# Top-k attention: the exponent moves into the evacuation of transposed blocks, GpSimd scales, scores are kept two pairs ahead

## The reference

```python
scores = jnp.einsum('bhnd,bhmd->bhnm', q, k) * DHEAD ** (-0.5)
kth = jax.lax.top_k(scores, TOPK)[0][..., -1:]            # TOPK = 64
masked = jnp.where(scores >= kth, scores, jnp.finfo(scores.dtype).min)
attn = jax.nn.softmax(masked, axis=-1)
o = jnp.einsum('bhnm,bhmd->bhnd', attn, v)
...
o = _conv1x1(o, Wo, bo) + x
```

## Time and profile before

| | us |
|---|---|
| median of 3 runs | 5220.38 |
| lowest and highest | 5220.33 and 5223.14 |
| span of the profiled execution, first to last instruction | 5216.1 |

### The profile page before, as it was taken

The page is one execution under the profiler, slowest core; times in us unless marked ns, Lnnn a source line. Parts: engine busy times, 40 slices in busy tenths (PEclk is TensorE's granted clock), DMA queues, the critical chain, the costliest instruction groups (busy, mean ns, idle before and its releaser), DMA issues. The chain is left out here.

```text
span 5216.1 us, 112540 instructions
## 1 busy us (share of the span) xinstructions
PE 4171.7 (80%) x32161; PEld 2822.7 (54%) x32161; DVE 4319.4 (83%) x25277; ACT 4144.4 (79%) x6082; POOL 1502.1 (29%) x362
## 2 busy tenths in 40 slices
PE   8576677776776667766777777898999999999999
PEld 4344445444444344444555445443567777777776
DVE  4899899998999899989999999531378888888886
ACT  2798799988998788988999889644267887778785
POOL 0344345443454344444444444200100000000000
PEclk9677777777777677767777777899899999999999
DMA  6000000000000000000000000200320101011112
GB/s 211 6 18 16 7 17 17 8 17 14 11 17 17 7 17 8 17 16 8 17 18 8 17 16 8 65 6 0 151 73 25 35 25 34 25 34 33 26 34 93
DMA packets 79613, 154.90 MB, mean 30 GB/s; under 512 B 8120, under 2 KB 49464, under 8 KB 73528
## 3 DMA queue, kind: packets, MB, share of 16 engines
q1 hardware_dynamic: 78904, 146.72, 9.8%
HBM read 99.50 MB, written 47.19 MB: 28 GB/s over the span
## 5 line engine op out<-in xcount | busy, mean ns | idle before, releaser
L542 POOL TENSOR_TENSOR a_probs<-a_scores,a_probs 128x2304 f32<-128x2304 f32 x288 | 1460.2, 5092 | 1728.3 <-ACT a_probs L465 1728.3
L560 DVE MAX8 a_top<-a_scores 128x8 f32<-128x36 f32 x18432 | 1831.1, 180 | 47.0 <-ACT a_scores L449 47.0
L376 PE MATMUL a_ps_t<-ident,a_probs 128*128 128x128 f32 x5184 | 974.7, 326 | 646.7 <-ACT a_probs_t L460 520.1
L376 PEld LDWEIGHTS a_ps_t<-ident,a_probs 128*128 128x128 f32 x5184 | 673.9, 164 | 934.5 <-ACT a_probs_t L460 656.4
L465 ACT ACTIVATE a_probs<-a_scores,a_steep_kth 128x2304 f32<-128x2304 f32 x290 | 641.2, 2211 | 242.3 <-DVE a_minus_max L696 242.3
L1159 PE MATMUL b_ps_t<-ident,b_soft 128*128 128x128 f32 x5184 | 748.4, 280 | 20.5 <-issue 18.6
L1284 DVE TENSOR_SCALAR_CACHE_REDUCE b_soft<-b_ps_s 128x2304 f32<-128x2304 f32 x288 | 735.3, 2553 | 28.4 <-PE b_ps_s L1143 10.4
L460 ACT ACTIVATE a_probs_t<-a_ps_t 128x512 f32<-128x512 f32 (+1 forms) x1440 | 726.9, 545 | 22.3 <-PE a_ps_t L376 7.9
L1159 PEld LDWEIGHTS b_ps_t<-ident,b_soft 128*128 128x128 f32 x5184 | 583.2, 142 | 205.7 <-issue 80.6
L1241 ACT ACTIVATE b_soft<-b_soft,b_minus_max 128x2304 f32<-128x2304 f32 x288 | 638.1, 2216 | 41.6 <-issue 24.4
L366 PE MATMUL a_ps_s<-a_k_stack,a_q_ring 128*128 128x512 f32 (+1 forms) x1465 | 651.7, 604 | 14.2 <-ACT a_scores L449 9.6
(11 more groups left out here) (134 smaller groups left out, 4149.7 us busy)
## 6 DMA issues: line engine op xcount, KB each, us to landing
a_k_stack<-k_parts SPq DMA_DIRECT2D x72, 288.0 KB, 6.0
b_k_stack<-k_parts SPq DMA_DIRECT2D x72, 288.0 KB, 6.0
a_q_ring<-q_parts SPq DMA_DIRECT2D x294, 64.0 KB
b_q_ring<-q_parts SPq DMA_DIRECT2D x294, 64.0 KB
k_parts<-p_high SPq DMA_DIRECT2D x36, 256.0 KB, 2.1
k_parts<-p_rest SPq DMA_DIRECT2D x36, 256.0 KB, 2.1
q_parts<-p_high SPq DMA_DIRECT2D x36, 256.0 KB, 2.0
q_parts<-p_rest SPq DMA_DIRECT2D x36, 256.0 KB, 2.0
```

The source lines that it names most:

```text
L376: last = pe.transpose(ps_t[(NTG * s + g) % 2][:, P * m:P * m + P], probs[s % 2][:, P * (m0 + m):P * (m0 + m) + P], cst["ident"][:, :])
L542: pool.tensor_tensor(probs[u][:, :], scores_all[:, 2 * (p % 2) + u, :], probs[u][:, :], ALU.subtract).then_inc(masked_ready, 1)
L560: last = dve.max(top8[s // 2 % 2][:, s % 2, c, :], scores_all[:, s % 4, CHUNK * c:CHUNK * c + CHUNK])
```

## The change

`exponentials` no longer works in place: GpSimd, after its mask, adds `minus_max` (now the plain negative maximum) and multiplies by SCALE in place, and signals `shifted_ready`; TensorE transposes that, and ScalarE's evacuation of a transposed group is an Exp instead of a Copy. The row's sum comes out of TensorE: `v_s` has 32 columns of ones beside V, so that `weigh` has 64 output columns, two neighbouring blocks write two halves of `ps_o`, and `add_quadrants` brings 33 columns, the last of which is the sum. `o_top` holds 33 columns a head, and `project_out` divides out of it into a new tile. Scores are made and kept two tiles further ahead: `score(s + 6)` and `(s + 7)` instead of `(s + 5)` and `(s + 6)`, `keep_scores(s + 6)` and `(s + 7)` at the end of ScalarE's iteration instead of `(s + 4)` and `(s + 5)` inside it. The counts of doubts move to unused columns of `ps_s`. The core of the diff:

```diff
-        v_s = [sb(f"v{n}", [P, MCH, D]) for n in range(2)]
+        v_s = [sb(f"v{n}", [P, MCH, 2 * D]) for n in range(2)]
...
-                    rows = slice(D * (m % 4), D * (m % 4) + D)
+                    rows = slice(2 * D * (m % 2), 2 * D * (m % 2) + 2 * D)
                     last = pe.matmul(ps_o[rows, P * (s % 2):P * (s % 2) + P], v_s[s // MCH][:, m, :], probs_t[:, m, :],
-                                     start=m < 4, stop=m + 4 >= MCH)
+                                     start=m < 2, stop=m + 2 >= MCH)
...
-                    last = pe.matmul(ps_o[:, O_COL + D * u:O_COL + D * u + D], parts[:, P * u:P * u + P],
+                    first = O_COL + (D + 1) * u
+                    last = pe.matmul(ps_o[:, first:first + D + 1], parts[:, P * u:P * u + P],
                                      cst["add_up"][:, :], start=True, stop=True)
...
             count_doubts(0)
+            score(5, 0, 5)
...
-                    pe.wait_ge(probs_ready, tile + 1)
+                    pe.wait_ge(shifted_ready, tile + 1)
                     turn(s, 0, tile)
                     turn(s, 1, tile)
-                    score(s + 5, h, tile + 5)
                     if p % PAIRS == 0:
                         pe.wait_ge(v_ready, h * B + p // PAIRS + 1)
                     pe.wait_ge(parts_ready, pair + 1)
                     weigh(s, 0, tile)
                     turn(s, 2, tile)
+                    weigh(s, 1, tile)
                     turn(s, 3, tile)
-                    weigh(s, 1, tile)
+                    score(s + 6, h, tile + 6)
+                    weigh(s, 2, tile)
                     turn(s, 4, tile)
-                    weigh(s, 2, tile)
                     weigh(s, 3, tile)
-                    pe.wait_ge(probs_ready, tile + 2)
+                    pe.wait_ge(shifted_ready, tile + 2)
                     turn(s + 1, 0, tile + 1)
                     weigh(s, 4, tile)
+                    turn(s + 1, 1, tile + 1)
+                    weigh(s + 1, 0, tile + 1)
+                    turn(s + 1, 2, tile + 1)
                     count_doubts(pair + 1)
-                    turn(s + 1, 1, tile + 1)
-                    turn(s + 1, 2, tile + 1)
-                    weigh(s + 1, 0, tile + 1)
+                    weigh(s + 1, 1, tile + 1)
                     turn(s + 1, 3, tile + 1)
-                    weigh(s + 1, 1, tile + 1)
+                    weigh(s + 1, 2, tile + 1)
                     turn(s + 1, 4, tile + 1)
-                    for g in range(2, NTG):
-                        weigh(s + 1, g, tile + 1)
+                    weigh(s + 1, 3, tile + 1)
+                    weigh(s + 1, 4, tile + 1)
                     add_quadrants(pair)
-                    score(s + 6, h, tile + 6)
+                    score(s + 7, h, tile + 7)
...
-            def keep_turned(s, g, tile):
+            def exponentials(s, g, tile):
+
                 m0, n = TGROUPS[g]
                 act.wait_ge(turned, tile * NTG + g + 1)
                 act.activation(probs_t[:, m0:m0 + n, :],
                                ps_t[(NTG * s + g) % 2][:, 0:n * P].rearrange("p (m q) -> p m q", q=P),
-                               ACT.Copy).then_inc(turned_kept, 1)
+                               ACT.Exp).then_inc(turned_kept, 1)
...
-                    exponentials(s, h, tile, parity)
-                    keep_scores(s + 4, tile + 4)
+                    exponentials(s, 0, tile)
                     guess_place(1, pair + 1, 1 - parity)
-                    keep_turned(s, 0, tile)
-                    keep_turned(s, 1, tile)
-                    exponentials(s + 1, h, tile + 1, parity)
-                    keep_turned(s, 2, tile)
-                    keep_turned(s, 3, tile)
-                    keep_turned(s, 4, tile)
-                    keep_scores(s + 5, tile + 5)
+                    exponentials(s, 1, tile)
+                    exponentials(s, 2, tile)
+                    exponentials(s, 3, tile)
+                    exponentials(s, 4, tile)
+                    exponentials(s + 1, 0, tile + 1)
+                    exponentials(s + 1, 1, tile + 1)
                     keep_any(pair + 1)
-                    keep_turned(s + 1, 0, tile + 1)
-                    keep_turned(s + 1, 1, tile + 1)
+                    exponentials(s + 1, 2, tile + 1)
+                    exponentials(s + 1, 3, tile + 1)
                     act.wait_ge(kth_ready, pair + 2)
                     penalty(0, 1 - parity)
-                    keep_turned(s + 1, 2, tile + 1)
-                    keep_turned(s + 1, 3, tile + 1)
-                    keep_turned(s + 1, 4, tile + 1)
+                    exponentials(s + 1, 4, tile + 1)
                     penalty(1, 1 - parity)
                     act.wait_ge(weighed, tile + MCH + 3)
                     act.activation(parts[:, :], ps_o[:, 0:PAIR], ACT.Copy).then_inc(parts_ready, 1)
                     guess_place(0, pair + 2, parity)
+                    wait_alone(act, masked_ready, tile + 3)
+                    keep_scores(s + 6, tile + 6)
                     finish(s, h, pair)
+                    wait_alone(act, masked_ready, tile + 4)
+                    keep_scores(s + 7, tile + 7)
...
                     for u in range(2):
-                        pool.wait_ge(penalty_ready, tile + u + 1)
+
+                        wait_alone(pool, penalty_ready, tile + u + 1)
                         pool.tensor_tensor(probs[u][:, :], scores_all[:, 2 * (p % 2) + u, :], probs[u][:, :],
                                            ALU.subtract).then_inc(masked_ready, 1)
+                        wait_alone(pool, masked_ready, tile + u + 1)
+                        pool.tensor_scalar(probs[u][:, :], probs[u][:, :], minus_max[p % 2][:, u:u + 1], SCALE,
+                                           ALU.add, ALU.mult).then_inc(shifted_ready, 1)
...
-                dve.tensor_tensor(o_c, o_c, inverse_c, ALU.mult).then_inc(divided, 1)
+                dve.tensor_tensor(o_c, o_heads[:, 4 * c:4 * c + 4, :, 0:D], inverse_c, ALU.mult).then_inc(divided, 1)
```

More of the change, by code:

```diff
@@ L84, in constants @@
         "ones": sb("ones", [P, P]),
-        "add_up": sb("add_up", [P, D]),
+        "add_up": sb("add_up", [P, D + 1]),
     }
-    made = ctx.enter_context(nc.semaphore("constants_made"))
+    made, zeroed = ctx.enter_context(nc.semaphore("constants_made")), ctx.enter_context(nc.semaphore("ident_zeroed"))
     Tally.semaphore = ctx.enter_context(nc.semaphore("waits_alone"))
@@ L92, in _ @@
         def _(pool):
-            pool.memset(k["ident"][:, :], 0.0).then_inc(made, 1)
-            pool.wait_ge(made, 1)
+            pool.memset(k["ident"][:, :], 0.0).then_inc(zeroed, 1)
+            pool.wait_ge(zeroed, 1)
             pool.affine_select(out=k["ident"][:, :], in_=k["ident"][:, :], compare_op=ALU.not_equal,
                                fill=1.0, base=0, pattern=[[-1, P]],
-                               channel_multiplier=1).then_inc(made, 1)
+                               channel_multiplier=1).then_inc(made, 2)
         @block.vector
@@ L101, in _ @@
             dve.memset(k["ones"][:, :], 1.0)
[L102 to L106, removed]
+            dve.memset(k["add_up"][:, :], 0.0).then_inc(made, 1)
+            dve.wait_ge(made, 3)
+            for half in range(2):
+                values, total = 2 * D * half, 2 * D * half + D
+                dve.tensor_copy(k["add_up"][values:values + D, 0:D], k["ident"][values:values + D, values:values + D])
+                dve.tensor_copy(k["add_up"][total:total + D, D:D + 1], k["ident"][total:total + D, total:total + 1])
     return k
@@ L309, in attention_top @@
         ps_o = ctx.enter_context(nc.psum_tensor("a_ps_o", [P, BANK], F32))
-        O_COL, FLAG_COL = PAIR, PAIR + 2 * D
+        flag_counts = ps_s[0:1, N:N + 3]
+        O_COL = PAIR
         v_ready = sem("v_ready")
@@ L318, in attention_top @@
         kth_ready = sem("kth_ready")
-        penalty_ready, masked_ready, probs_ready = sem("penalty_ready"), sem("masked_ready"), sem("probs_ready")
+        penalty_ready, masked_ready, shifted_ready, ones_set = (sem("penalty_ready"), sem("masked_ready"),
+                                                                sem("shifted_ready"), sem("ones_set"))
         turned, turned_kept = sem("turned"), sem("turned_kept")
@@ L392, in count_doubts @@
                 pe.wait_ge(doubt_ready, pair + 1)
-                pe.matmul(ps_o[0:1, FLAG_COL:FLAG_COL + 2], cst["ones"][:, 0:1], doubt[:, :], start=True, stop=True)
+                pe.matmul(flag_counts[:, 0:2], cst["ones"][:, 0:1], doubt[:, :], start=True, stop=True)
                 for u in range(2):
-                    last = pe.matmul(ps_o[0:1, FLAG_COL + 2:FLAG_COL + 3], cst["ones"][:, 0:1], doubt[:, u:u + 1],
+                    last = pe.matmul(flag_counts[:, 2:3], cst["ones"][:, 0:1], doubt[:, u:u + 1],
                                      start=u == 0, stop=u == 1)
@@ L498, in _ @@
             act.wait_ge(kth_ready, 1)
```

(15 more changed lines are left out.)

25 lines of the change are left out of this document (13 added, 12 removed).

## The result

The changed kernel takes 6484.3 us (median of four runs, 6481.2 to 6488.9) against 5221.8 for the kernel before: a ratio of 1.242, 95% interval 1.240 to 1.244. The span of the profiled execution is 6482.1 us. The prediction was 6650, its range 5900 to 7250.

A forecast was written before the change was run, and what follows sets the result against it. ScalarE and VectorE, both nearly full, were taken to bound the kernel before; after, a ring through GpSimd's masks. 9.9 us times 143 pairs plus 10 for the start, added to 5220, gave about 6650 us, range 5900 to 7250.

The forecast's parts named there:

- the ring: Attention loop: GpSimd's masks and the TensorE-ScalarE exchange take turns, as late keepings wait for masks; 30.75 us a pair against 20.82.
- Step 1: From the end of penalty(0), GpSimd does mask 0, scale 0 and mask 1 while ScalarE ends up waiting: 13.15 us.
- Step 2: ScalarE after mask 1: keep_scores(s+7), exponentials(s,0), guess_place, exponentials(s,1), with scale 1 running under it: 4.3 us.
- Step 3: TensorE alternates turns and weighs up to turn(s+1,3), plus a score and count_doubts: 9.0 us at full clock, 13.3 at half.
- 10 for the start: The first iteration of the loop also waits for mask 1: about 10 us, once.
- 1.26 were carried: Mean pair minus ordinary pair before the change, from pairs counted again: 1.26 us, 180 us in all, taken as unchanged.
- Step 4: ScalarE's exponentials(s+1,3) with its handover, then penalty(0), before GpSimd's next mask: 3.0 us.
- Signs: In the changed profile: ScalarE idle 6 to 7 us a pair, GpSimd 13 to 15, evacuations 1.1 to 2 us apart.
- Hidden work: VectorE's select and the threshold some 2 us later end about level with TensorE's exchange; other added work under 1 us.
- GpSimd's scale is not dear: Denies the rival that GpSimd's scale costs 10.8 us, making 41 us a pair and 8100 us in all; chance 0.08.
- Exchange at ScalarE's own work: Rival: evacuations overlap with TensorE's exchange and take only ScalarE's busy time, 23.9 to 26 us a pair, 5660 to 5960; chance 0.08.
- VectorE setting the pace and winning: Rival: mask waits are over before ScalarE reaches them, VectorE's 19.7 us sets the pair, 5105 us; chance 0.05.

The follow-up runs named there:

- turns_ahead_no_scale: turns_ahead without GpSimd's scale: SCALE goes into ScalarE's Exp, the shift by the row's largest score is left out; 5167.4 us, 0.990 of the kernel before.
- scores_as_before: The changed kernel with scores made and kept at the places of the kernel before, all else as changed; 5650.5 us, 1.083 of the kernel before.
- turns_ahead: scores_as_before with TensorE turning two groups ahead of the weighing and penalty(0) two evacuations earlier; 5644.8 us, 1.082 of the kernel before.
- before_scores_ahead: The kernel before with only the scores made and kept two pairs ahead, as in the change; 6084.5 us, ratio 1.166.
- before_spare_op: The kernel before plus one unneeded GpSimd subtract of 128x2304 in every pair, on a tile nobody else uses; 5689.5 us, ratio 1.091.

## Why the prediction was right

The forecast, its sign and its mechanism held: the ring that the moved keeping closes sets the pace. Its terms, against the pair shown:

- *Step 1*, 13.15: from the end of `penalty(0)` to the end of mask 1, 12.68 us (2006.73 to 2019.41). The scale is 2.185 us, not 2.7, inside the bounds of 1.9 to 5.1. Taken alone, that is 74 of the 166 us by which the forecast was high. The lower bound was worked out wrong: (0.671 - 0.204) x 4 leaves out the fixed part itself, and with it the same two rows give 2.07, nearer than any price that was put. GPSIMD Engine Reference of the Trainium skill, section Engine selection, calls one-input work roughly line-rate; the estimate from it, 1.9, was also nearer than the copy's row. A wait of GpSimd for its own preceding instruction costs 0.21 us.
- *Step 2*, 4.3: 4.1 us, from 2019.41 to 2023.52.
- *Step 3*, 9.0 to 13.3: 9.4 us, from there to the evacuation at 2032.88. The clock was 0.51 at first and 1.00 later, as expected. That 9.4 lies so close to the quick end is partly luck: turns and weighs took some 7.9 us and not 6.4, since the first of them ran at the lower clock, and the score, put at 2.27 in both bounds of the step, took about 1.2 at the higher. TensorE's scores of this place in three pairs in a row:

```profile
2025.90 1.29 PE L370 MATMUL a_ps_s<-a_k_stack,a_q_ring 128*128 128x512 f32 x5
...
2055.09 1.88 PE L370 MATMUL a_ps_s<-a_k_stack,a_q_ring 128*128 128x512 f32 x5
...
2084.86 2.27 PE L370 MATMUL a_ps_s<-a_k_stack,a_q_ring 128*128 128x512 f32 x5
```

Step 3 takes 9.4, 10.2 and 10.6 us in these pairs, and the pairs 28.9, 29.8 and 30.2; steps 1, 2 and 4 agree within 0.1. So 17.6 for steps 2 to 4, which is 16.3 in the pair shown, was nearly right for the usual one (29.83 - 12.68 = 17.15). The median pair, 29.83 against 30.75, makes 132 of the 166 us; the rest is 10 for the start and 1.09 us between mean and median where 1.26 were carried.

- *Step 4*, 3.0: 2.8 us, from 2032.88 to 2035.67.
- *Signs.* ScalarE waits 1.90 + 5.22 = 7.1 us a pair for the mask (6 to 7 forecast), GpSimd 14.05 and 15.23 for `penalty` (13 to 15); two of these lie just over the upper end. From 2024.43 on the evacuations start 0.96 to 2.00 us apart (1.1 to 2). In a stretch of 28.9 us ScalarE is busy 15.84 and VectorE 19.34, 55% and 67%: the half and the two thirds (busy times as in the earlier trace rows, after the length).

```profile
2004.50:2033.40 28.90, 17.70 (x131) 12.86 (x129) 19.34 (x161) 15.84 (x26) 14.48 (x4) 0.76 0.22 46
```

- *Hidden work.* Level with step 3, as said, but the threshold follows `select` by more than the 2 us put. VectorE:

```profile
2028.75 0.16 DVE L631 SCALAR_TENSOR_TENSOR a_doubt<-a_beyond,a_kth 128x2 f32<-128x2 f32 x1
...
2033.18 0.17 DVE L710 TENSOR_SCALAR a_steep_kth<-a_kth 128x2 f32<-128x2 f32 x1 [3.09 <-issue]
2033.25 0.17 DVE L711 TENSOR_SCALAR a_minus_max<-a_extremes 128x2 f32<-128x2 f32 x1
```

`select` ends at 2028.9 and `hand_on` comes 4.3 us later. It waits for `keep_any` (2031.70), and that for `count_doubts`, which stands among the turns and weighs in TensorE's list. The threshold is there at 2033.4, and `penalty(0)` starts at 2033.45. So exchange and threshold end together, and both go through TensorE. The recounts cost about what they did: 19 of the same length.

The rivals: GpSimd's scale is not dear (2.185 against 10.8). Exchange at ScalarE's own work did not come: six of the ten evacuations wait for a turn, 0.36 to 1.40 us. VectorE setting the pace and winning did not come with this change, but is what turns_ahead_no_scale shows (VectorE busy 41.33 of 45.00 us from 1700 to 1745), some 60 us above the 5105 given for it.

One thing the argument lacked, without being punished for it: it priced GpSimd's added instructions in the ring alone. In the changed kernel `select` starts after scale 1 has ended (2023.17 against 2021.80), so the two do not meet. Where the ring is opened they do, and the scale costs 419 us again by holding VectorE. scores_as_before came out at the time that the ring gave, but its factor too takes 2.20 us in the mean, so that hit does not show the ring; turns_ahead, with a shorter ring and the same time, speaks against the ring as what set the pace there. The ring of the change rests on its own rows and on before_scores_ahead, where the factor is not held (0.17 us, row of 1714.80).

## What to carry to other kernels

Before a producer is moved ahead, look whose slot it overwrites: if that slot's last reader stands late in the same iteration, the move ties two engines into a ring, however much work it takes off either. When an idle engine is given work, ask what it shares with the engine that sets the pace, and at which moment it will run. And where two engines are both nearly full, relieving one is worth at most the slack of the other: ScalarE lost 595 us of busy time in the best version, and the time fell by 50.

## What the runs showed of the hardware that was not expected

A VectorE instruction on two elements a row can wait until the GpSimd instruction under way has ended: in the rows shown 2.0 to 3.7 us instead of 0.17, ending within 0.04 us of it. In before_spare_op 128 of the 144 factors were held, and each ended 0.02 to 0.04 us after the subtract. Not all kinds are held: in turns_ahead 108 MAX8 take 10.58 us (1701.10), most of it under a mask and a scale, 98 ns each, and a TENSOR_SCALAR with accumulator (1716.45) takes 0.44 us under the scale, as in the kernel before (0.436 in the mean). SBUF — State Buffer of the Trainium skill, section Who interferes with whom, has the rule: VectorE and GpSimd share a pair of ports, which goes to whoever issues first, for the whole instruction; instructions with two inputs in SBUF and the two-port modes want it, one-input instructions outside these modes and the accumulating form do not. The runs agree: `beyond`, `guess` and the factor were held, MAX8 and the accumulating form were not. That the factor, a one-input instruction, ran in a two-port mode is what the rule would need; no run here shows the mode.

A price per element does not carry over between GpSimd's instructions: 2304 elements a row took 5.07 us for the mask, 4.03 for the spare subtract of a tile from itself, and 2.185 for the scale.
